# One last stage for epilogue and routed layer, and changed orders in self attention and the upward projection of a two-layer decoder

## The chip, the cores and the metric

The kernel runs on one core of a Trainium2 chip, as one launch. The metric is the device time of the execution in microseconds (us), the median of several runs of the same program. The engines are TensorE (PE in the rows; PEld is its weight load), VectorE (DVE), ScalarE (ACT), GpSimd (POOL) and SyncE (SP), which issues the DMAs. Each runs its own queue in order, and they wait for one another by semaphores.

## The reference, cut to what matters

The input x is 16 x 128 x 1024, and six sublayers follow one another, each with its residual and a layer norm:

```
x = _layernorm(x + _L0_attn_ref(x, ...))      # hydra: down, gelu, two mixers, gate, up
x = _layernorm(x + _L0_xattn_ref(x, ctx, ...))
x = _layernorm(x + _L0_ffn_ref(x, ...))
x = _layernorm(x + _L1_attn_ref(x, ...))      # self attention, rotary, 32 heads, 8 kv heads
x = _layernorm(x + _L1_xattn_ref(ctx, x, ...))# recurrent decoder over 128 steps
x = _layernorm(x + _L1_ffn_ref(x, ...))       # routed layer with a sign matrix
```

Of these, the diff touches the following lines:

```
alpha = jax.nn.sigmoid(gate1)                       # hydra's end
h = alpha * xmid + (1.0 - alpha) * h
h = xmid + h
h = h @ w_up.T + b_up
return x_init + jnp.transpose(h, (1, 0, 2))

att = jnp.where(causal, q k / sqrt(d), -inf)        # self attention, per head
out = (softmax(att) @ v) @ Wo

y = jnp.tanh(g @ L_gy_w.T + L_gy_b + s @ L_sy.T) @ L_yy_w.T + L_yy_b   # decoder, per step

routing = softmax(xf @ gate_w.T)                    # routed layer
out = xf * (routing @ in_channel_scale) @ sign(weight).T * (routing @ out_channel_scale) + bias
```

In the decoder, s and g of each step come from a recurrence; y depends on them alone, so it is made for all steps after the recurrence.

## The kernel before, in words

X, the 16 tiles of 128 rows x 1024, stays in SBUF through the whole kernel; a tile is one sequence, b from 0 to 15. PSUM is one tensor `ps` of eight banks of 512 floats. The stages follow one another. Each is a block in which every engine has a queue written out by hand; where a block ends, all engines meet, the stage's semaphores are cleared and all meet again (`Scope.release`, L48). `Chain` (L21) lets an engine wait for its own instruction by a semaphore.

All sublayers end in `Norm` (L64): VectorE forms the row (sum of product and X), `statistics` makes its mean and variance in three operations (L96, L99), GpSimd's `factors` makes scale and shift in four small ones (L106 to L109), and ScalarE's `apply` (L113) writes the normalised row to X. There are two row buffers; `row_free` counts the applied tiles (plus two).

**Hydra's end, L294 to L742.** The block "mx" (L295 on) runs two mixer layers. Its ScalarE begins with one exponential (L484), its VectorE with the setup of taps (L638 to L646), and then waits for TensorE's first projections. The block "up" (L677 on) makes the gate from `gate1` (ScalarE L690, VectorE L722 to L725), scales u (L726), mixes all sixteen tiles in one operation (L727) into `hm`, and then TensorE multiplies each tile by `w_up` and adds the bias (L712, L149), two banks for each tile in turn. VectorE forms the rows (L738).

**Self attention, L1287 to L1638.** For a tile b, TensorE (L1454 on) makes: scores of head group 0, the query projection of tile b+1 group 0, scores of group 1, query projection group 1, then for c = 0: four turns of probabilities (`turn_probs`, L1415, two banks in turn, 4 transposes each), `attend` (L1423); then the key (L1393) and value (L1398) projections of tile b+1; then `turn_probs` and `attend` for c = 1, the turned rows of tile b+2, and the output projection (L1438). ScalarE copies each turned piece out of PSUM (`keep_probs`, L1507), makes the exponentials (L1499) and copies keys and values (`keep_kv`, L1491 and L1492). `turn_probs` waits until the piece two before it is copied; `attend` until all four are.

**The decoder's epilogue, L2199 to L2269.** With all states `sh` and alignments `ah` kept, TensorE makes the tanh's arguments for four tiles at a time (L2218, L2221), ScalarE the tanh (L2241, into `hy`), and then for each tile TensorE makes y (L2229, two halves, with a bias product L149) into two banks, VectorE adds X (L2266), and the norm follows.

**The routed layer, L2277 to L2550.** For each tile: GpSimd copies the row out of X (L2349) and adds the bias to the copy (L2356), which waits for the row of the tile before; TensorE transposes the copy (L2375); the router's logits, softmax and a transposed routing follow (L2383 to L2507); input scales are a small product (L2399); VectorE multiplies (L2511), and three bf16 parts are split off in turn by ScalarE (L2458, L2460) and VectorE (L2514, L2516). The layer is 24 products for each half of 512 columns (L2412), into banks 4 and 5; the output scales (L2421) go to banks 6 and 7 and are kept by ScalarE (L2486). VectorE forms the row by L2542 and L2544 and only then (L2545) frees banks 4 and 5 and the bias rows. TensorE's order for tile b is: turned rows of b+1, output scales of b, route b+1, first half layer (with logits and turned routes of b+1 in it), input scales of b+1, second half layer. ScalarE's order is: output scales of b kept (L2486), split of b+1, kept rows and exponentials of b+2, `apply` of b. Before the loop ScalarE takes the sign of the eight weight tiles (L2477), which eight DMAs bring (L2335), and TensorE waits for all eight.

Of the kernel before, what the change touches and what calls it, by code (L numbers as in the profile page):

```python
# [163 lines left out]
def stage_hydra(nc, X, ps, ident, a):  # L164
    with ExitStack() as ctx:
# [128 lines left out]
        with ExitStack() as inner:  # L294
# [31 lines left out]
                "sq_done ssq_done rs_done rs_ready spread o_done o_kept u_done")  # L326
            UNITS = 4 * CH + 2
            CONV = (2 * CH, 2 * CH + 1)
            BANK = 4
            with nc.Block() as block:  # L330
# [306 lines left out]
                def _(dve):  # L637
# [10 lines left out]
                    dve.wait_ge(a_done, 1)  # L648
# [27 lines left out]
        with ExitStack() as inner:  # L676
# [4 lines left out]
            load, e_done, dve_seq, pool_seq, mixed, summed, freed = t.sems(  # L681
                "load e_done dve_seq pool_seq mixed summed freed")
            with nc.Block() as block:
# [4 lines left out]
                @block.scalar  # L688
                def _(act):
                    act.activation(gate[:, 1:2], gate[:, 0:1], ACT.Exp, scale=-1.0).then_inc(e_done, 1)  # L690
# [27 lines left out]
                def _(dve):  # L718
                    dve.wait_ge(e_done, 1)
                    link = Chain(dve, dve_seq)  # L720
                    al = gate[:, 2:3]
                    link(dve.tensor_scalar(al, gate[:, 1:2], 1.0, None, ALU.add))  # L722
                    link(dve.reciprocal(al, al))
                    link(dve.tensor_scalar(gate[:, 3:4], al, -1.0, 1.0, ALU.mult, ALU.add))
                    link(dve.tensor_scalar(al, al, 1.0, None, ALU.add))  # L725
                    link(dve.tensor_scalar(u[:, :], u[:, :], gate[:, 3:4], None, ALU.mult))  # L726
                    dve.scalar_tensor_tensor(out=hm[:, :, :].rearrange("p t s -> p s t"),  # L727
                                             in0=xmid[:, :].rearrange("p (s t) -> p s t", t=SEQ), scalar=al,
                                             in1=u[:, :].rearrange("p (s t) -> p s t", t=SEQ),
                                             op0=ALU.mult, op1=ALU.add).then_inc(mixed, 1)  # L730
# [1918 lines left out]
```

## Time and profile before

| | us |
|---|---|
| median of 3 runs (3503.76 to 3507.91) | 3505.43 |
| profiled execution, its own time | 3504.24 |
| its span | 3502.4 |
| upward projection, first product to last normalised row | 241.89 to 301.1 |
| self attention | 806 to 1595 |
| decoder's recurrence, up to its last operation | to 3153.8 |
| epilogue, first DMA to last normalised row | 3155.1 to 3226.9 |
| routed layer, first instruction to the end | 3228.0 to 3502.4 |

```
PE 3034.8 (87%) x42733; PEld 2061.2 (59%) x42778; DVE 1974.6 (56%) x5167; ACT 1699.7 (49%) x4978; POOL 288.1 (8%) x994
```

The shares are averages over stages with different limits: in each place that the change touches, what counts is which wait ends last there. The span is from the first to the last instruction; 1.8 us of the execution lie around it. In the timelines of the section below, a row has the start, the length, the engine, the line, the operation, output and inputs, shapes and count, and in brackets the idle time before it and what ended it. "L12" is line 12 of the kernel. A float32 product shows as two records.

### The profile page before, as it was taken

Reading aid. Unit: us, or ns where it says so; the run is one execution under the profiler, and the core shown is the slowest. Engines: PE = TensorE matmul, PEld = TensorE weight load, DVE = VectorE, ACT = ScalarE, POOL = GpSimd, SP = SyncE. Lnnn points to the kernel's source line nnn. Section 1 sums busy time; section 2 is a strip of 40 time slices with the busy share of each in tenths; the row PEclk is TensorE's granted clock in tenths of the full one; section 3 lists DMA queues with packets and bytes.
Section 4 is the critical chain, followed back from the end, with each engine's and each line's share of the span. In section 5 each row is a group of like instructions: output and inputs, shape, how many; then the busy total and the mean of one; then the engine's idle time right before and its main releaser. Section 6 shows DMA issues by size and latency. Waiting matters only on the chain. (4 is left out here: it accounts for less than half of the span.)

```text
span 3502.4 us, 107527 instructions
## 1 busy us (share of the span) xinstructions
PE 3034.8 (87%) x42733; PEld 2061.2 (59%) x42778; DVE 1974.6 (56%) x5167; ACT 1699.7 (49%) x4978; POOL 288.1 (8%) x994
## 2 busy tenths in 40 slices
PE   7876985667999999988989999999999999996898
PEld 4434552336777667754457677676767767762444
DVE  3776776885555555552035555555555555555454
ACT  2333544553444444441136666666666666653433
POOL 1002000000000000001000000000000000002232
PEclk8988997888999999999999999999999999998899
DMA  3002002001000000001123333333333333321100
GB/s 114 8 7 61 11 5 87 0 0 51 1 0 0 0 0 0 0 1 64 35 55 93 88 93 89 91 92 89 93 88 93 88 93 88 93 83 39 49 36 36
DMA packets 287962, 176.19 MB, mean 50 GB/s; under 512 B 23574, under 2 KB 277095, under 8 KB 287901
## 3 DMA queue, kind: packets, MB, share of 16 engines
q1 hardware_dynamic: 284860, 171.16, 16.7%
q0 software_dynamic: 3040, 4.23, 0.6%
q8 instruction: 37, 0.61, 0.1%
q14 instruction: 25, 0.20, 0.0%
HBM read 164.36 MB, written 14.16 MB: 51 GB/s over the span
## 5 line engine op out<-in xcount | busy, mean ns | idle before, releaser
L1987 PE MATMUL ps<-de_hg,st_at 128*32 128x128 f32 x16384 | 516.3, 275 | 0.3 <-DVE st_at L2148 0.3
L1987 PEld LDWEIGHTS ps<-de_hg,st_at 128*32 128x32 f32 x16384 | 424.4, 110 | 31.6 <-DVE st_at L2148 0.5
L2052 ACT ACTIVATE st_th<-ps,st_sw 128x128 f32<-128x128 f32 x1024 | 291.9, 368 | 237.5 <-PE ps L1959 237.5
L2131 DVE TENSOR_TENSOR st_th<-ps,st_sw 128x512 f32<-128x512 f32 x256 | 177.1, 692 | 162.3 <-PE ps L1959 162.3
L1380 PE MATMUL ps<-sa_xt,w_wq 128*128 128x128 f32 x2048 | 239.3, 278 | 0.8 <-ACT sa_xt L1481 0.8
L1380 PEld LDWEIGHTS ps<-sa_xt,w_wq 128*128 128x128 f32 x2048 | 233.5, 194 | 4.9 <-issue 1.4
L1948 PE MATMUL ps<-st_hk,de_cwt 112*32 112x128 f32 x4096 | 164.7, 278 | 79.7 <-DMA st_hk<-padded_alignments 76.1
L1438 PE MATMUL ps<-sa_wo,sa_ct 128*128 128x512 f32 x512 | 222.6, 593 | 0.0
L1499 ACT ACTIVATE sa_pr<-sa_pr,sa_nm 128x128 f32<-128x128 f32 x512 | 197.6, 389 | 7.6 <-DVE sa_nm L1585 7.6
L1959 PE MATMUL ps<-st_fs,de_waf 32*128 32x128 f32 x4096 | 186.5, 296 | 15.8
L2412 PE MATMUL ps<-rf_wb,rf_sp 128*128 128x512 bf16 x737 | 175.3, 385 | 16.9 <-DVEq L2545 15.3
L1948 PEld LDWEIGHTS ps<-st_hk,de_cwt 112*32 112x32 f32 x4096 | 100.2, 109 | 144.8 <-ACT st_gt L2071 94.3
L2125 DVE COPY ps<-de_enc 128x512 f32<-128x512 f32 x256 | 175.1, 684 | 5.9 <-PE ps L2021 5.9
L2162 DVE TENSOR_TENSOR st_rec<-ps,st_rin 128x128 f32<-128x128 f32 x256 | 74.7, 292 | 176.2 <-PE ps L1987 176.2
L1925 POOL COPY de_ah<-st_at 128x8 f32 (+1 forms) x256 | 50.7, 198 | 1444.1 <-DVE st_at L2148 1444.1
L1974 PE MATMUL ps<-st_th,st_vas 128*32 128x128 f32 x4096 | 165.3, 279 | 1.7 <-ACT st_th L2057 1.7
L1629 DVE TENSOR_TENSOR sa_row<-ps,X 128x512 f32<-128x512 f32 x32 | 22.1, 692 | 254.5 <-PE ps L1438 254.5
L2057 ACT ACTIVATE st_th<-st_th 128x512 f32<-128x512 f32 x256 | 165.2, 645 | 0.0
L1438 PEld LDWEIGHTS ps<-sa_wo,sa_ct 128*128 128x128 f32 x512 | 96.0, 190 | 116.5 <-issue 116.5
L2045 ACT COPY ps<-de_enc 128x512 f32<-128x512 f32 x256 | 156.8, 612 | 10.0 <-PE ps L2021 10.0
L1959 PEld LDWEIGHTS ps<-st_fs,de_waf 32*128 32x128 f32 x4096 | 137.7, 185 | 33.9 <-ACT st_fs L2042 30.5
L113 ACT ACTIVATE X<-sa_row,sa_rs_ln 128x1024 f32 (+1 forms) x16 | 19.9, 1242 | 274.5 <-POOL sa_rs_ln L109 274.5
(400 smaller groups left out, 5816.1 us busy)
## 6 DMA issues: line engine op xcount, KB each, us to landing
st_hk<-padded_alignments SPq DMA_DIRECT2D x254, 448.0 KB, 3.6
X<-in_x_dram SPq DMA_DIRECT2D x16, 512.0 KB, 8.1
out_dram<-X SPq DMA_DIRECT2D x16, 512.0 KB, 2.6
w_wq<-in_Wq_perm_dram SPq DMA_DIRECT2D x1, 4096.0 KB
sa_wo<-in_Wo_perm_dram SPq DMA_DIRECT2D x1, 4096.0 KB, 14.2
gate_inputs<-dp_ro SPq DMA_DIRECT2D x16, 256.0 KB, 2.3
st_rin<-gate_inputs SPq DMA_DIRECT2D x128, 32.0 KB, 3.2
rf_wf<-in_weightT_dram SPq DMA_DIRECT2D x8, 512.0 KB, 6.9
```

Of the source, the lines that this page charges most:

```text
L1380: ins = pe.matmul(ps[:, 6 + c, g * P:(g + 1) * P], wq[:, k, (4 * c + g) * P:(4 * c + g + 1) * P], xt[:, k, :], start=(k == 0), stop=(k == ...
L1438: ins = pe.matmul(ps[:, 6 + h, :], ct[:, k // 4, (k % 4) * P:(k % 4 + 1) * P], wo[:, k, h * 512:(h + 1) * 512], start=(k == 0), stop=(k == ...
L1499: ins = act.activation(pr[:, c, h, :], pr[:, c, h, :], ACT.Exp, bias=nm[:, c, h:h + 1], accum_out=sums[:, c, h:h + 1])
L1948: ins = pe.matmul(F[g][32 * j:32 * j + 32, :], cwt[:, i, :], hk[g][:, 2 * j + i, :], start=(i == 0), stop=(i == 1), tile_position=(0, 32 * ...
L1959: ins = pe.matmul(ps[:, j, c0:c0 + P], waf[32 * j:32 * j + 32, i, :], fs[g][32 * j:32 * j + 32, :], start=False, stop=True, tile_position= ...
L1974: ins = pe.matmul(E[g][32 * j:32 * j + 32, :], vas[:, i, :], th[g][:, 2 * j + i, :], start=False, stop=(i == 1), tile_position=(0, 32 * j) ...
L1987: ins = pe.matmul(R[g][32 * q:32 * q + 32, :], at[g][:, b, :], hg[:, BG * g + b, q * P:(q + 1) * P], start=False, stop=(b == BG - 1), tile ...
L2052: ins = act.activation(th[g][:, b, :], sums(g, 0)[:, b // 2, (b % 2) * P:(b % 2 + 1) * P], ACT.Tanh, bias=sw[g][:, b:b + 1])
L2057: act.activation(v, v, ACT.Tanh).then_inc(th_done[g], 1)
L2125: dve.tensor_copy(sums(g, 1), four(enc[:, BG * g + 4:BG * g + 8, :])).then_inc(filled1[g], 1)
L2131: dve.tensor_tensor(th[g][:, 4:8, :].rearrange("p (k s) n -> p k s n", s=2), sums(g, 1).rearrange("p k (s n) -> p k s n", s=2), sw[g][:, 4 ...
L2412: ins = pe.matmul(ps[:, 4 + h, :], sp3[:, k, part, m * P:(m + 1) * P], wb[:, m, h * 512:(h + 1) * 512], start=(n == 0), stop=(n == 3 * KH ...
```

## The change

It has four parts.

1. The gate. The exponential of the gate moves to the head of the block "mx" on ScalarE, and its four small VectorE operations with it, ahead of the two layers. There xmid is scaled by 1 + alpha, once. In "up", the scaling of u and the single mix are replaced by four operations of four tiles each, and TensorE waits for the one that it needs.
2. Self attention. `turn_probs` is split, and the projections of tile b+1 stand between its parts; ScalarE's copies are put in the same order.
3. Epilogue and routed layer are one stage. State products, tanh and the first three y tiles (AHEAD = 3) come first; the further y tiles are made inside the routed loop, three tiles ahead, between the input scales and the second half layer, in banks 6 and 7. A second `Norm` (`eln`) has its own rows. The weights `wf` have room for four tiles, and the last four DMAs wait for a sign each. The large decoder tensors are released before the stage, in a release of their own. TensorE's loop over the tiles is written out.
4. GpSimd's copy of a row and its bias addition are split, with the factors of the y row three ahead between them, and the copy waits until that tile's y row is applied.

The diff, cut to its core (indentation-only lines left out):

```diff
@@ mx, ScalarE and VectorE @@
 act.activation(nega[:, :], alog[:, :], ACT.Exp).then_inc(a_done, 1)
+act.activation(gate[:, 1:2], gate[:, 0:1], ACT.Exp, scale=-1.0).then_inc(a_done, 1)
...
-dve.wait_ge(a_done, 1)
+dve.wait_ge(a_done, 2)
+link(dve.tensor_scalar(al, gate[:, 1:2], 1.0, None, ALU.add))
+link(dve.reciprocal(al, al))
+link(dve.tensor_scalar(gate[:, 3:4], al, -1.0, 1.0, ALU.mult, ALU.add))
+link(dve.tensor_scalar(al, al, 1.0, None, ALU.add))
+link(dve.tensor_scalar(xmid[:, :], xmid[:, :], al, None, ALU.mult))
@@ up @@
-pe.wait_ge(mixed, 1)
 for b in range(NB):
+    pe.wait_ge(mixed, b // 4 + 1)
...
-link(dve.tensor_scalar(u[:, :], u[:, :], gate[:, 3:4], None, ALU.mult))
-dve.scalar_tensor_tensor(out=hm[:, :, :].rearrange("p t s -> p s t"),
...
+for c in range(CH):
+    rows = slice(4 * c, 4 * c + 4)
+    dve.scalar_tensor_tensor(out=hm[:, rows, :].rearrange("p t s -> p s t"),
...
@@ self attention, TensorE @@
-turn_probs(pe, b, 0, n0)
-attend(pe, b, k, 0, n0)
-if more:
-    for c in range(NC):
-        project_k(pe, b + 1, c)
-    project_v(pe, b + 1)
-turn_probs(pe, b, 1, n0 + QD)
+for c in range(NC):
+    turn_probs(pe, b, 0, n0, range(2 * c, 2 * c + 2))
+    if more:
+        project_k(pe, b + 1, c)
+attend(pe, b, k, 0, n0)
+turn_probs(pe, b, 1, n0 + QD, range(2))
+if more:
+    project_v(pe, b + 1)
+turn_probs(pe, b, 1, n0 + QD, range(2, QD))
 attend(pe, b, k, 1, n0 + QD)
@@ self attention, ScalarE @@
 keep_context(act, b, 0)
+keep_probs(act, b, 1, n0 + QD, range(2))
 if more:
     keep_kv(act, b + 1, 1 - k)
-keep_probs(act, b, 1, n0 + QD)
+keep_probs(act, b, 1, n0 + QD, range(2, QD))
@@ routed stage, SyncE @@
+for dst, src in ((lsy, "L_syT"), (gyb, "L_gy_b"), (lyy, "L_yyT")):
+    sp.dma_start(dst[:, :], a[src]).then_inc(yy_load, 16)
...
 for k in range(KH):
-    sp.dma_start(wf[:, k, :], a["weightT"][k * P:(k + 1) * P, :]).then_inc(wf_load[k // 2], 16)
+    if k == 4:
+        sp.dma_start(bias[:, :], a["bias"].partition_broadcast(P)).then_inc(bias_load, 16)
+    if k >= 4:
+        sp.wait_ge(signed, k - 3)
+    sp.dma_start(wf[:, k % 4, :], a["weightT"][k * P:(k + 1) * P, :]).then_inc(wf_load[k // 2], 16)
@@ GpSimd @@
+eln.start_pool(pool, link)
+ln.start_pool(pool, link)
+for b in range(2):
+    eln.factors(pool, link, b, b)
+for b in range(2):
+    stage_rows(b, b)
+eln.factors(pool, link, 2, 0)
+for b in range(2):
+    add_bias(b, b)
+def body(b, k, more):
+    link = state["link"]
+    if has(b + 2):
+        stage_rows(b + 2, k)
+    if has(b + AHEAD):
+        eln.factors(pool, link, b + AHEAD, 1 - k)
+    if has(b + 2):
+        add_bias(b + 2, k)
+    ln.factors(pool, link, b, k)
@@ TensorE @@
+def make_y(pe, b):
+    pe.wait_ge(hy_done, b // 4 + 1)
+    if b >= 2:
+        pe.wait_ge(y_used, b - 1 if b == 2 else b)
+    if b >= AHEAD:
+        pe.wait_ge(os_kept, b - AHEAD + 1)
+    for h in range(2):
+        out = ps[:, y_bank(b) + h, :]
+        pe.matmul(out, hy[:, b, :], lyy[:, h * 512:(h + 1) * 512], start=True, stop=False)
+        ins = y_bias.add(pe, out, h)
+    ins.then_inc(y_rows, 1)
...
     if more:
         input_scales(pe, b + 1, 1 - k)
+    if b + AHEAD < NB:
+        make_y(pe, b + AHEAD)
     layer(pe, b, k, 1)
@@ ScalarE @@
+eln.apply(act, 0, 0)
+eln.apply(act, 1, 1)
 keep_rows(act, 0)
+signs(range(0, 2))
 exps(act, 0)
+signs(range(2, 4))
 split(act, 0, 0)
+eln.apply(act, 2, 0)
+signs(range(4, KH))
...
     ln.apply(act, b, k)
+    if has(b + AHEAD):
+        eln.apply(act, b + AHEAD, 1 - k)
@@ VectorE @@
+def y_row(dve, link, b, k):
+    n = y_bank(b) if isinstance(b, int) else 6
+    dve.wait_ge(y_rows, b + 1)
+    eln.wait_free(dve, b)
+    link(dve.tensor_tensor(eln.row[:, k, :], ps[:, n:n + 2, :].rearrange("p a n -> p (a n)"), tile_of(b), ALU.add))
+    dve.sem_inc(y_used, 1)
...
 dve.tensor_tensor(r1[:, :], ys[:, :], sp3[:, k, 0, :], ALU.subtract).then_inc(r_done, 1)
+if between is not None:
+    between()
...
-        scale_rows(dve, link, b + 1, 1 - k)
+        ahead = has(b + AHEAD)
+        scale_rows(dve, link, b + 1, 1 - k, (lambda: y_row(dve, link, b + AHEAD, 1 - k)) if ahead else None)
+        if ahead:
+            eln.statistics(dve, link, 1 - k)
```

## Rows read from the trace of the kernel before

**Rows 1.** Busy time by stretch: epilogue, and routed loop; columns name start:end and length first.

```profile
3172.40:3221.20 48.80, 34.97 (x89) 12.89 (x88) 42.30 (x76) 17.36 (x14) 14.98 (x57) 0.99 0.00 0
3283.00:3473.00 190.00, 176.73 (x1244) 94.71 (x1269) 108.15 (x169) 75.80 (x116) 56.37 (x77) 1.00 0.09 36
```

**Rows 2.** One tile of the routed loop: timeline; last its rows' DVE group.

```profile
3270.84 1.89 PE L2412 MATMUL ps<-rf_wb,rf_sp 128*128 128x512 bf16 x7 [0.85 <-DVEq L2545]
3270.85 2.35 POOL L2356 TENSOR_TENSOR rf_xb<-rf_xs,rf_bias 128x1024 f32<-128x1024 f32 x1 [19.26 <-DVEq L2545]
3274.51 1.24 ACT L113 ACTIVATE X<-rf_row,rf_rs_ln 128x1024 f32 x1 [1.07 <-POOL rf_rs_ln L109]
3275.66 0.99 ACT L2486 COPY rf_os<-ps 128x1024 f32<-128x1024 f32 x1
3276.36 0.73 PE L2399 MATMUL ps<-rf_rT,rf_ics 8*128 8x128 f32 x16
3277.01 5.35 PE L2412 MATMUL ps<-rf_wb,rf_sp 128*128 128x512 bf16 x23
3277.15 1.23 DVE L2511 TENSOR_TENSOR rf_ys<-ps,rf_xt 128x1024 f32<-128x1024 f32 x1 [1.26 <-PE ps L2399]
3279.56 1.23 DVE L2514 TENSOR_TENSOR rf_r<-rf_ys,rf_sp 128x1024 f32<-128x1024 f32 x1 [1.18 <-ACT rf_sp L2458]
3283.04 1.22 DVE L2542 TENSOR_TENSOR rf_row<-ps,rf_os 128x1024 f32<-128x1024 f32 x1
L2542 DVE TENSOR_TENSOR rf_row<-ps,rf_os x16: 1217/1218/1225, 3268.2 to 3491.4; 128x1024 f32<-128x1024 f32 x16
```

**Rows 3.** Head of the upward projection: timeline, and the weights' DMA (last: us to landing).

```profile
238.04 3.70 DVE L727 SCALAR_TENSOR_TENSOR up_hm<-hy_xmid,hy_gate,hy_u 128x2048 f32<-128x2048 f32 x1
241.89 2.04 PE L712 MATMUL ps<-up_w_up,up_hm 128*128 128x512 f32 x2 [10.96 <-DVE up_hm L727]
up_w_up<-in_w_upT_dram SPq DMA_DIRECT2D x1, 512.0 KB, 4.1
```

**Rows 4.** Timeline of one self-attention tile, TensorE: start us, us.

```profile
1095.26 1.04 PE L1419 MATMUL ps<-identity,sa_pr 128*128 128x128 f32 x8
1099.48 3.84 PE L1393 MATMUL ps<-sa_xt,w_wk 128*128 128x128 f32 x32
1106.61 1.04 PE L1419 MATMUL ps<-identity,sa_pr 128*128 128x128 f32 x8
1109.83 1.06 PE L1427 MATMUL ps<-sa_pt,sa_vv 128*32 128x512 f32 x8 [0.68 <-ACT sa_pt L1507]
```

**Rows 5.** The same tile, ScalarE timeline.

```profile
1107.34 1.09 ACT L1507 COPY sa_pt<-ps 128x512 f32<-128x512 f32 x2
```

**Rows 6.** Timeline of the epilogue's first tiles.

```profile
3172.10 1.02 PE L2229 MATMUL ps<-yy_lyy,yy_hy 128*128 128x512 f32 x2
3173.18 1.02 PE L2229 MATMUL ps<-yy_lyy,yy_hy 128*128 128x512 f32 x2
3173.78 1.42 DVE L96 BATCH_NORM_STATS2 yy_stats<-yy_row 128x6 f32<-128x512 f32 x2
3175.52 1.22 DVE L2266 TENSOR_TENSOR yy_row<-ps,X 128x1024 f32<-128x1024 f32 x1
3179.68 0.19 POOL L109 TENSOR_TENSOR yy_rs_ln<-yy_vy,yy_rs_ln 128x1 f32<-128x1 f32 x1
```

**Rows 7.** Timeline behind a stage that ends with two releases.

```profile
302.77 1.28 ACT L889 ACT_TABLE_LOAD   x1 [1.68 <-PEq L51]
```

**Rows 8.** Timeline of the routed layer's head, from its first row copy.

```profile
3228.49 1.04 POOL L2349 COPY rf_xs<-X 128x1024 f32<-128x1024 f32 x1
3244.73 3.89 ACT L2477 ACTIVATE rf_wb<-rf_wf 128x1024 bf16<-128x1024 f32 x4
3248.96 1.96 PE L2375 MATMUL ps<-identity,rf_xs 128*128 128x128 f32 x8 [11.32 <-ACT rf_wb L2477]
```

**Rows 9.** Timeline at the last tile, TensorE.

```profile
3479.07 12.21 PE L2412 MATMUL ps<-rf_wb,rf_sp 128*128 128x512 bf16 x47 [2.21 <-DVEq L2545]
```

More of the change, by code:

```diff
@@ L680, in stage_hydra @@
             ln = Norm(t, X)
-            load, e_done, dve_seq, pool_seq, mixed, summed, freed = t.sems(
-                "load e_done dve_seq pool_seq mixed summed freed")
+            load, dve_seq, pool_seq, mixed, summed, freed = t.sems(
+                "load dve_seq pool_seq mixed summed freed")
             with nc.Block() as block:
@@ L1412, in scores, with turn_probs @@
                 ins.then_inc(s_sum, 1)
-            def turn_probs(pe, b, c, n0):
-                for r in range(QD):
+            def turn_probs(pe, b, c, n0, rs):
+                for r in rs:
                     pe.wait_ge(normed, QD * (2 * b + c) + r + 1)
@@ L1501, in exps, with keep_probs @@
                     ins.then_inc(exp_done, 1)
-            def keep_probs(act, b, c, n0):
-                for r in range(QD):
+            def keep_probs(act, b, c, n0, rs):
+                for r in rs:
                     act.wait_ge(tp_done, n0 + r + 1)
@@ L2315, in over_tiles @@
         def over_tiles(eng, body, start=lambda i: None):
-            with eng.Fori(0, NB // 2 - 1) as i:
+            with eng.Fori(0, NB // 2 - 2) as i:
                 start(i)
@@ L2319, in over_tiles, with has @@
                 body(2 * i + 1, 1, True)
-            start(NB // 2 - 1)
-            body(LAST - 1, 0, True)
-            body(LAST, 1, False)
+            start(NB // 2 - 2)
+            for b in range(NB - 4, NB):
+                body(b, b % 2, b < LAST)
+        def has(b):
+            return not isinstance(b, int) or b <= LAST
         with nc.Block() as block:
@@ L2347, in stage_rows, with add_bias @@
                         pool.wait_ge(biased, b - 1)
-                    if not (isinstance(b, int) and b == 1):
-                        pool.tensor_copy(xs[:, k, :], tile_of(b)).then_inc(staged, 1)
+                    pool.wait_ge(eln.row_free, b + 3)
+                    pool.tensor_copy(xs[:, k, :], tile_of(b)).then_inc(staged, 1)
+                def add_bias(b, k):
                     if not (isinstance(b, int) and b < 2):
                         pool.wait_ge(row_done, b - 1)
+                    else:
+                        pool.wait_ge(bias_load, 16)
@@ L2352, in stage_rows @@
                     pool.wait_ge(staged, b + 1)
-                    if isinstance(b, int) and b == 0:
-                        pool.tensor_copy(xs[:, 1, :], tile_of(1)).then_inc(staged, 1)
-                        pool.wait_ge(bias_load, 16)
                     pool.tensor_tensor(xb[:, k, :], xs[:, k, :], bias[:, :], ALU.add).then_inc(biased, 1)
-                ln.start_pool(pool, Chain(pool, pool_seq))
-                stage_rows(0, 0)
-                stage_rows(1, 1)
-                with pool.Fori(0, NB // 2 - 1) as i:
-                    link = Chain(pool, pool_seq, ln.POOL_SETUP + i * 2 * ln.POOL_LINKS)
-                    for k in range(2):
-                        stage_rows(2 * i + k + 2, k)
-                        ln.factors(pool, link, 2 * i + k, k)
@@ L2370, in turn_rows, with start @@
+                state = {}
+                def start(i):
+                    state["link"] = Chain(pool, pool_seq, SETUP + i * 4 * ln.POOL_LINKS)
+                over_tiles(pool, body, start)
             def turn_rows(pe, b, k):
@@ L2435, in _ @@
                 pe.wait_ge(signed, KH)
-                def body(b, k, more):
+                pe.wait_ge(y_used, AHEAD)
+                for b in range(NB):
+                    k, more = b % 2, b < LAST
                     if more:
@@ L2488, in body @@
                         split(act, b + 1, 1 - k)
-                    if not isinstance(b, int) or b < LAST - 1:
+                    if has(b + 2):
                         keep_rows(act, b + 2)
@@ L2521, in _ @@
                 dve.memset(rt[:, :, :], 0.0).then_inc(cleared, 1)
+                dve.wait_ge(yy_load, 48)
+                dve.tensor_scalar(lsy[:, :], lsy[:, :], 0.5, None, ALU.mult).then_inc(halved, 1)
                 link = Chain(dve, dve_seq)
+                for b in range(AHEAD):
+                    y_row(dve, link, b, b % 2)
+                    eln.statistics(dve, link, b % 2)
                 softmax_top(dve, 0)
```

1057 lines of the change are left out of this document (508 added, 549 removed).

## The prediction

> **What bounds the kernel now.** I read the timeline of each place that the diff touches, and the busy times by stretch for its clock. In the epilogue stage VectorE is busy for 42.30 of 48.80 us [rows 1]: a tile costs it a row addition and statistics, while TensorE only makes two short products, so tiles pass at VectorE's pace. In the routed loop TensorE is busy for 176.73 of 190.00 us at a granted clock of 1.00, and VectorE for 108.15 [rows 1]; the starts of the sixteen row multiplications, 3268.2 to 3491.4, are (3491.4 - 3268.2) / 15 = 14.88 us apart [rows 2]. In each tile TensorE waits 0.85 us for the row of the tile before [rows 2]. So one stage leaves TensorE room and the other leaves room to VectorE and ScalarE; to run them together is worth what the slower engine of each hides. In self attention TensorE bounds, and what can go is only its waits for ScalarE's copies. In the upward projection the first product stands still until one operation of 3.70 us has mixed all sixteen tiles [rows 3].
>
> **Upward projection.** Before, the first product starts at 241.89, behind the mix that starts at 238.04 [rows 3]. After, the gate's five small operations and the scaling of xmid are done in the mixing stage, and the mix is four operations, of which the first takes about 3.70 / 4 = 0.93 us. The product then waits for its weights: they are asked for at the stage's start, 234.4, and land 4.1 us later [rows 3], at 238.5. Gain 241.89 - 238.6 = 3.3 us; the rest of that stage is paced by VectorE as before and moves with it. The moved operations stand in VectorE's queue ahead of its first convolution, which waits for a projection of TensorE; I cost them at nothing, since TensorE has to run two groups of projections first. Without that cover they cost some 2 us. Bounds: 0 (quartered rows are costly, or that cover is gone) to 3.9 (the weights earlier).
>
> **Self attention, fifteen tiles.** From the first turned probabilities at 1095.26 to the second attend at 1109.83 a tile takes 14.57 us [rows 4]. TensorE's work in it is four pairs of turns at 1.03 and one attend at 1.0 (1.04 and 1.06 in the rows, less what the next one overlaps), and the key and value projections, 1106.61 - 1099.48 = 7.13 [rows 4]: 12.25 us. The waits are 2.32. The new order puts one key projection (1.8) between the first two pairs of turns, the other before the attend, and the value projection between the last two. Each is longer than the 1.09 us of a pair of copies [rows 5], so three of four waits go. What stays is the last: ScalarE copies keys and values, then two pieces of probabilities. In the trace this string ends at 1107.34 + 1.09 = 1108.43, that is 1.82 after the value projection's issue ends at 1106.61 [rows 4, 5]; TensorE has only one pair of turns (1.03) to fill it and some 0.1 for the semaphore, an estimate: it waits 1.82 + 0.1 - 1.03 = 0.89. Gain 2.32 - 0.89 = 1.43 a tile, 15 x 1.43 = 21.3 (the last tile has no projections). ScalarE now waits for the third turn behind the key projection, so the exponentials behind it come about 2 us later; the value projection gives their consumer more room than that. Bounds: 0.5 a tile (they are late after all) to 2.32, that is 8 to 35 us.
>
> **Tail, the head of the new stage.** The state products and the first two y rows run as before. The first row copy of the routed layer can follow the second tile's factors, which end at 3179.68 + 0.19 = 3179.87 [rows 6]; an added release ahead of the stage, bounded by nothing and by the 1.68 us that ScalarE sat behind two of them [rows 7], I take at 0.4. So the copy starts at 3180.3 where it was at 3228.49 [rows 8]: 48.2 us earlier. From the copy to the loop it was 3248.96 - 3228.49 = 20.5 us [rows 8], a string of ScalarE's copies, splits and eight signs (the last four 3.89). I keep that length: weights now land under the y rows, which removes a wait, and the third row's normalisation of 1.24 comes in. The last four weight tiles wait for a sign each, with more than 10 us before their use; SyncE's stores of the result, queued behind them, begin only with the first finished row. A table for tanh that lacks the exponential or the sign would add a load of 1.28 [rows 7]. Bounds 17 to 24.
>
> **Tail, the loop.** Call H the start of a tile's first half layer, 3270.84 [rows 2]. The y product adds two halves of 3173.18 - 3172.10 = 1.08 us [rows 6], so 2.15, behind the input scales, which end at 3276.36 + 0.73 = H + 6.25. It also waits until ScalarE has kept the output scales, for they share two banks. That copy starts at 3275.66, H + 4.82, and takes 0.99 [rows 2]. Ahead of it in ScalarE's queue there is now one more normalisation of 1.24 (the same operation at 3274.51 [rows 2]), so it ends at H + 7.05. The y product starts at H + 7.1, a new wait of 0.9, and ends at H + 9.25; the second half layer of 5.35 [rows 2] ends at H + 14.6, and VectorE's row can start at H + 14.74. VectorE's own string: before, its row starts at 3283.04, H + 12.20 [rows 2]. Put in are the y row, which the epilogue shows at 1.22 [rows 6] and which with its own semaphore I take at 1.37; it begins when the subtraction at 3279.56 ends and covers the wait for the cast (the last operation comes 0.27 later); and a tile's statistics, 3175.52 - 3173.78 = 1.74 [rows 6]: H + 14.21. So TensorE's side is last by half a us. From row to next H it is 14.88 - 12.20 = 2.68, and the period is 14.74 + 2.68 = 17.42, 2.54 more. Twelve tiles pay that; the first, where no normalisation stands ahead of that copy, pays 2.0; the last three pay nothing. Together 32.5. Bounds per tile: 2.0 (no wait for the copy) to 3.6 (a row copy of 1.04 on top). GpSimd's queue gets a second set of factors between its copy and its bias addition; that addition starts with the row at H anyway [rows 2], and the factors are ready two us earlier. The added release at the end: 0.4, same bounds.
>
> **The page that speaks against it.** GpSimd's row copy, 1.04 us [rows 8], now waits for the normalised y row and falls at H + 6.2 to H + 7.2; VectorE's subtraction with two SBUF inputs starts at 3279.56, H + 8.7 [rows 2]. They are 1.5 us apart; no row shows the two together. The Trainium skill (SBUF — State Buffer, section "SBUF: two separate sides") says that GpSimd and such an operation of VectorE exclude one another for the whole instruction. By that the sum stays, as long as ScalarE is not 1.5 us later than I work out; if it is, rival B below.
>
> **Sum.** -3.3 - 21.3 - 48.2 + 32.5 + 0.4 = -39.9. The profiled execution took 3504.24 us (span 3502.4), so 3464.3; the median of the runs lies 1.2 above it: 3465.5 us.
>
> **Rivals.** *A, no wait for the output scales:* ScalarE's normalisations come earlier than I think. Against it: the tile's normalisation waits for GpSimd, whose bias addition of 2.35 starts at H [rows 2]. 12 x (2.54 - 2.01) = 6.4 less: 3459. *B, the copy and the subtraction meet:* 13 x 1.04 = 13.5 more: 3479. For it: ScalarE's queue is longer by 1.24 in each tile. *C, self attention gains only 8:* the later exponentials delay the last two normalised pieces. Against it: they have the whole value projection, over 3 us, as room. 13 more: 3479. *D, self attention loses all its waits:* 0.89 x 15 = 13.4 less: 3452. Against it the string of four copies above. *E, slower:* TensorE's clock falls in the loop. A pause of 0.85 leaves it at 1.00 [rows 1, 2]; behind the pause of 2.21 at the last tile 47 matmuls took 12.21 [rows 9] where two halves at the loop's pace are 10.7, so one fall costs 1.5. If both pauses of a tile (before the y product and before H) grow to 2.2, a tile pays 1.3 + 1.9 of pause and 3.0 of clock, 13 x 6.2 = 81 more: 3546. It decides from 39.9 / 13 = 3.1 us a tile. Against it: I find pauses of 0.9 and 0.3. *F, an edit does not take effect:* the upward product waits elsewhere, or the quarter mixes are slow: 3469.
>
> **How the numbers follow.** Forecast 0.48, A 0.12, B 0.12, C 0.12, D 0.05, E 0.05, F 0.06. The likeliest gives 3465.5. The range 3450 to 3486 takes in A to D and F, A with D for its lower end (3446 is left out) and B or C with a head at its long bound for its upper; E and mixtures of the rest are outside. A measurement of this kernel can tell about 0.2%, 7 us, from no change. Every case but E is faster by more; with something for a mixture that ends near zero: faster 0.92, within 0.02, slower 0.06.
>
> **What would show it.** In self attention the waits of the attend on the copies halve, to about 0.9 a tile, and the tile is 1.4 shorter. The first upward product starts near 238.6, released by its DMA. The first row copy of the routed layer is near 3156, where the earlier stages' 25 us are off. Routed rows 17.4 apart, with a wait of 0.9 ahead of the y product, released by ScalarE's copy of the output scales; 16.9 would be A, 18.5 B. A clock below 1.00 in the loop would be E. If the tile of self attention keeps its length, the order was not what cost.

## The result, and the profile after

The changed kernel takes **3460.55 us** (median of 4 runs, 3457.25 to 3462.39); the kernel before, run beside it, 3506.67 (4 runs, 3503.76 to 3514.15). The ratio is 0.9864, 95% interval 0.9848 to 0.9880: about 46 us faster. The forecast was 3465.5, in a range from 3450 to 3486. The profiled execution took 3461.36 us with a span of 3459.6, against 3504.24 and 3502.4.

The difference of the two spans, 42.8 us, by marks that both traces have (a set-up operation at the start of the mixing stage, the first transfer of each later stage, the last product of the decoder recurrence with the state weights):

| stretch | before | after | difference |
|---|---|---|---|
| start to the mixing stage | 65.8 | 62.8 | -3.0 |
| mixing stage | 168.6 | 167.9 | -0.7 |
| upward projection to the start of self attention | 575.4 | 572.6 | -2.8 |
| self attention and what follows, to the recurrence | 970.9 | 944.1 | -26.8 |
| decoder recurrence, 128 steps | 1367.7 | 1376.4 | +8.7 |
| recurrence to the first transfer of the tail | 6.7 | 7.1 | +0.4 |
| tail, from there to the end | 347.3 | 328.7 | -18.6 |

Two of these lie where no edit is: the 3.0 us ahead of the mixing stage, and 8.7 us lost in the recurrence. The experiments come back to both. The lines of the changed kernel are shifted by a few; the text names operations.

**Upward projection.** Timeline of its head in the kernel after (start us, us, engine, line, operation, output<-input, in brackets the idle time before and what ended it); it answers to [rows 3]:

```profile
230.74 0.37 SPq L695 DMA_DIRECT2D up_w_up<-in_w_upT_dram  x1
230.79 3.86 DVE L729 SCALAR_TENSOR_TENSOR up_hm<-hy_u,hy_gate,hy_xmid 128x512 f32<-128x512 f32 x4 [1.06 <-PEq L51]
234.46 2.08 PE L720 MATMUL ps<-up_w_up,up_hm 128*128 128x512 f32 x2 [7.22 <-DMA up_w_up<-in_w_upT_dram]
```

The four quarter mixes take 3.86 us together, 0.16 more than the one of 3.70 did. The product is now released by its weights and starts 3.72 us after they are asked for (234.46 - 230.74).

**Self attention.** Timeline of one tile, TensorE and the last copies of ScalarE; it answers to [rows 4, 5]:

```profile
1079.86 1.04 PE L1421 MATMUL ps<-identity,sa_pr 128*128 128x128 f32 x8
1080.73 2.02 PE L1395 MATMUL ps<-sa_xt,w_wk 128*128 128x128 f32 x16
1082.58 1.04 PE L1421 MATMUL ps<-identity,sa_pr 128*128 128x128 f32 x8
1083.46 1.95 PE L1395 MATMUL ps<-sa_xt,w_wk 128*128 128x128 f32 x16
1085.34 1.06 PE L1429 MATMUL ps<-sa_pt,sa_vv 128*32 128x512 f32 x8
1086.33 1.09 PE L1421 MATMUL ps<-identity,sa_pr 128*128 128x128 f32 x8
1087.26 3.62 PE L1400 MATMUL ps<-w_wv,sa_xt 128*128 128x256 f32 x16
1090.72 1.04 PE L1421 MATMUL ps<-identity,sa_pr 128*128 128x128 f32 x8
1091.45 1.09 ACT L1511 COPY sa_pt<-ps 128x512 f32<-128x512 f32 x2
1092.60 1.07 PE L1429 MATMUL ps<-sa_pt,sa_vv 128*32 128x512 f32 x8 [0.84 <-ACT sa_pt L1511]
```

The stretch that was 14.57 us is 12.74 (1092.60 - 1079.86), and one bracket is left in it: 0.84 us ahead of the second attend, behind the copies that end at 1092.54.

**Tail.** Timeline of the head; it answers to [rows 6 to 8]. The second line is the first row of the former epilogue, the third the first row copy of the routed layer, the last the start of the loop:

```profile
3130.87 1.28 ACT L2474 ACT_TABLE_LOAD   x1 [1.68 <-PEq L51]
3147.08 1.23 DVE L2532 TENSOR_TENSOR yy_row<-ps,X 128x1024 f32<-128x1024 f32 x1 [11.33 <-PE ps L149]
3154.29 1.04 POOL L2301 COPY rf_xs<-X 128x1024 f32<-128x1024 f32 x1
3170.55 3.88 ACT L2486 ACTIVATE rf_wb<-rf_wf 128x1024 bf16<-128x1024 f32 x4
3174.48 1.97 PE L2345 MATMUL ps<-identity,rf_xs 128*128 128x128 f32 x8 [9.68 <-ACT rf_wb L2486]
```

The one table load of the tail is that first line: the table serves tanh, exponential and sign alike. Between the row copy and the loop stand these, in order of time (GpSimd's two bias additions, the last two operations of VectorE's softmax, and ScalarE's first cast, which starts the split of the tile):

```profile
3157.87 4.65 POOL L2309 TENSOR_TENSOR rf_xb<-rf_xs,rf_bias 128x1024 f32<-128x1024 f32 x2
3160.49 0.17 DVE L2522 RECIPROCAL rf_ri<-rf_sm 128x1 f32<-128x1 f32 x1 [0.42 <-ACT rf_ex L2470]
3160.69 1.86 DVE L2523 TENSOR_SCALAR rf_rt<-rf_ex,rf_ri 128x32 f32<-128x32 f32 x1
3166.12 1.04 ACT L2461 CAST rf_sp<-rf_ys 128x1024 bf16<-128x1024 f32 x1 [3.77 <-DVE rf_ys L2537]
```

VectorE's scaling of the softmax takes 1.86 us here and 0.24 in every other tile and in the kernel before. It ends at 3162.55, GpSimd's additions at 3162.52. Next, one tile of the loop, which answers to [rows 2], and the group of its sixteen rows:

```profile
3267.75 1.89 PE L2382 MATMUL ps<-rf_wb,rf_sp 128*128 128x512 bf16 x8 [0.22 <-DVEq L2582]
3271.43 1.24 ACT L113 ACTIVATE X<-rf_row,rf_rs_ln 128x1024 f32 x1 [1.08 <-POOL rf_rs_ln L109]
3272.58 1.23 ACT L113 ACTIVATE X<-yy_row,yy_rs_ln 128x1024 f32 x1
3273.71 0.99 ACT L2503 COPY rf_os<-ps 128x1024 f32<-128x1024 f32 x1
3273.97 1.04 POOL L2301 COPY rf_xs<-X 128x1024 f32 x1 [2.67 <-ACT X L113]
3274.84 1.10 PE L2419 MATMUL ps<-yy_lyy,de_hgy 128*128 128x512 f32 x2 [0.85 <-ACT rf_os L2503]
3276.46 1.22 DVE L2540 TENSOR_TENSOR rf_r<-rf_ys,rf_sp 128x1024 f32<-128x1024 f32 x1 [1.18 <-ACT rf_sp L2461]
3277.07 5.34 PE L2382 MATMUL ps<-rf_wb,rf_sp 128*128 128x512 bf16 x24
3282.45 1.22 DVE L2579 TENSOR_TENSOR rf_row<-ps,rf_os 128x1024 f32<-128x1024 f32 x1 [0.67 <-PE ps L2382]
L2579 DVE TENSOR_TENSOR rf_row<-ps,rf_os x16: 1217/1224/1226, 3195.7 to 3448.4; 128x1024 f32<-128x1024 f32 x16
```

With H = 3267.75 the y product waits 0.85 us for ScalarE's copy of the output scales and starts at H + 7.09; the row starts at H + 14.70, with 0.67 us of room for VectorE. The forecast had H + 7.1 and H + 14.74. The thirteenth row starts at 3403.83, so twelve periods take (3403.83 - 3195.70) / 12 = 17.34 us each. The busy times of 200 us of this loop (stretch, length, busy us of PE, PEld, DVE, ACT, POOL, granted clock, DMA share, GB/s; compare [rows 1]):

```profile
3213.00:3413.00 200.00, 188.56 (x1233) 97.46 (x1232) 128.46 (x209) 82.27 (x118) 64.78 (x118) 1.00 0.08 32
```

TensorE is busy for 94% of it at a granted clock of 1.00 (the 2.4 GHz level): rival E did not come.

### The profile page after: what moved, and what is told of

It reads as the page before. It is cut to its first block and busy times, and to the rows that moved or that the text cites. A ratio compares the mean times of both kernels' runs of the same rounds, so it can differ in the third digit from the quotient of the medians.

```text
span 3459.6 us, 107419 instructions
## 1 busy us (share of the span) xinstructions
PE 3027.8 (88%) x42778; PEld 2061.6 (60%) x42778; DVE 1975.7 (57%) x5170; ACT 1693.2 (49%) x4976; POOL 288.2 (8%) x994
## 5 line engine op out<-in xcount | busy, mean ns | idle before, releaser
L1994 PE MATMUL ps<-dm_hg,st_at 128*32 128x128 f32 x16384 | 516.3, 275 | 0.3 <-DVE st_at L2155 0.3
L1994 PEld LDWEIGHTS ps<-dm_hg,st_at 128*32 128x32 f32 x16384 | 424.5, 110 | 31.6 <-DVE st_at L2155 0.5
L1955 PE MATMUL ps<-st_hk,dm_cwt 112*32 112x128 f32 x4096 | 164.7, 278 | 87.1 <-DMA st_hk<-padded_alignments 83.8
L1966 PE MATMUL ps<-st_fs,dm_waf 32*128 32x128 f32 x4096 | 186.5, 296 | 14.0
L1955 PEld LDWEIGHTS ps<-st_hk,dm_cwt 112*32 112x32 f32 x4096 | 100.3, 109 | 152.1 <-ACT st_gt L2078 104.9
L2132 DVE COPY ps<-dm_enc 128x512 f32<-128x512 f32 x256 | 175.0, 684 | 5.9 <-PE ps L2028 5.9
L2052 ACT COPY ps<-dm_enc 128x512 f32<-128x512 f32 x256 | 156.8, 613 | 10.1 <-PE ps L2028 10.1
L1966 PEld LDWEIGHTS ps<-st_fs,dm_waf 32*128 32x128 f32 x4096 | 137.7, 185 | 30.9 <-ACT st_fs L2049 26.5
```

The source lines that it names most:

```text
L1955: ins = pe.matmul(F[g][32 * j:32 * j + 32, :], cwt[:, i, :], hk[g][:, 2 * j + i, :], start=(i == 0), stop=(i == 1), tile_position=(0, 32 * ...
L1966: ins = pe.matmul(ps[:, j, c0:c0 + P], waf[32 * j:32 * j + 32, i, :], fs[g][32 * j:32 * j + 32, :], start=False, stop=True, tile_position= ...
L1994: ins = pe.matmul(R[g][32 * q:32 * q + 32, :], at[g][:, b, :], hg[:, BG * g + b, q * P:(q + 1) * P], start=False, stop=(b == BG - 1), tile ...
L2132: dve.tensor_copy(sums(g, 1), four(enc[:, BG * g + 4:BG * g + 8, :])).then_inc(filled1[g], 1)
```

## Experiments

### The three parts alone

The kernel before with one stage's edit each: the self attention order; the mixing stage and upward projection; the merged last stage with the freed arrays of the recurrence. Each takes the diff's hunks of its stage as they stand.

> Only the order in self attention is changed. My theory: that stage alone is 27 us shorter, as the kernel after shows, of which the first forecast took 21, so the time is near 3479 (ratio 0.9923), and the decoder recurrence is as in the kernel before (1367.6 us). Rival: the stage carries a part of what the other edits gave, and alone it is worth the forecast 21 us (0.9939).

**Measured:** 3475.87 us against 3501.32, ratio 0.9920 (0.9905 to 0.9935). From the first transfer of self attention to the recurrence it took 943.8 us (970.9 before). The stage earns its 27 us alone.

> Only the mixing stage and the upward projection are changed. My theory: the first upward product is released by its weights near 4 us after the stage starts (3.72 in the kernel after) instead of 7.5, the stage from its start to the start of cross attention takes 64.3 us instead of 68.3, and the run is about 4 us faster (ratio 0.9989), with the decoder recurrence as before (1367.6 us from its weight load to its last filter product). Rival: the 3.0 us by which the kernel after is already ahead when the mixing starts come from the change too, and the run is 7 us faster. Second rival: later stages wait for something else and give it back, 0 to 2 us faster.

**Measured:** 3501.58 us against 3501.32, ratio 0.9999 (0.9990 to 1.0008). In its profile the first product starts 3.7 us after the stage's first transfer, and from that transfer to self attention it took 570.5 us. The whole runs spread over 12 us for the kernel before alone (3495.39 to 3507.98); their interval leaves room for a gain of at most 3.5 us, so the forecast of 4 for the whole missed. The stage shows more: over all profiles of this study that stretch took 574.1 to 576.4 us in the six without the edit (mean 575.7) and 569.7 to 572.6 in the eight with it (mean 571.4). The edit is worth 4.3 us there. A part seems to be given back behind self attention, as the second rival has it: from the last normalised row of that stage to the first transfer of the recurrence the six took 188.8 to 189.0 us, and the eight 189.0 to 189.1 in three cases and 190.5 to 191.4 in five (mean 190.2, so 1.4 more). That would leave 2.9 of the 4.3 us, which the whole runs allow. Why those five are longer was not tried. Of the first rival the profiles leave nothing: the mixing stage began at 59.6 to 65.9 us and took either about 164 or about 168 us, with the edit and without.

> Only the merged last stage, with the arrays of the decoder recurrence freed ahead of it. My theory: from the end of the recurrence to the end the kernel takes 330.4 us instead of 348.6, so 18 us faster; the recurrence, whose instructions are unchanged, takes as long as in the kernel before, and its 8.7 us more in the kernel after was a variation of its transfers from run to run: ratio 0.9948. Rival: the changed placement of the arrays costs the recurrence the 8.7 us, and the run is only 9 to 10 us faster (0.9973).

**Measured:** 3481.78 us against 3501.32, ratio 0.9940 (0.9926 to 0.9953). The tail took 329.1 us from its first transfer, the recurrence 1369.1. Together the three ratios make 0.9860, the whole change 0.9864: the parts add up.

### Half of the self attention order

The kernel with the new order, but:

```
-                    for c in range(NC):
-                        turn_probs(pe, b, 0, n0, range(2 * c, 2 * c + 2))
-                        if more:
-                            project_k(pe, b + 1, c)
+                    turn_probs(pe, b, 0, n0, range(QD))
                     attend(pe, b, k, 0, n0)
+                    if more:
+                        for c in range(NC):
+                            project_k(pe, b + 1, c)
```

> Half of the self attention order: the first four turns of probabilities stay together ahead of their attend, both key projections follow it, and only the value projection lies between the two last pairs of turns. My theory: the wait of the first attend for ScalarE's copies stays, the waits inside the second four turns go, and the stage is 12 to 16 us shorter than before instead of 27. Rival: ScalarE's string is what bounds the tile, one place for the copies is as good as the other, and nearly all of the 27 us is there already; or nothing, because the string only moves into the second attend.

**Measured:** 3494.86 us, ratio 0.9980 (0.9970 to 0.9989); 964.2 us to the recurrence, so 6.7 less than before. The waits of TensorE from 900 to 1500 us, some thirteen tiles; first the kernel before, then this one, then the kernel after (what waited <- for what: us in total, times, longest):

```profile
PE ps L1427 <- ACT sa_pt L1507: 18.6, 26, 0.8
PE ps L1419 <- ACT sa_pt L1507: 8.4, 26, 0.4
```

```profile
PE ps L1427 <- ACT sa_pt L1509: 20.8, 26, 0.8
PE ps L1419 <- ACT sa_pt L1509: 3.8, 13, 0.3
```

```profile
PE ps L1429 <- ACT sa_pt L1511: 11.0, 13, 0.8
```

All three theories miss: 6.7 us is neither 12 to 16, nor nearly 27, nor nothing. Before, a tile waits (18.6 + 8.4) / 13 = 2.08 us; with the value projection moved 1.89; with the key projections moved too 0.85. The value projection takes one wait of 0.3 away ahead of a pair of turns, and the attend behind it still waits: the string of four copies comes after it in either order. With the value projection moved, moving the key projections brings the other 20 of the 27 us; they were not moved alone.

### The last wait of the self attention tile

The first half of the output projection's first column half needs only the first context, which has been kept by then:

```
                     turn_probs(pe, b, 1, n0 + QD, range(2, QD))
+                    project_out(pe, b, not more, True)
                     attend(pe, b, k, 1, n0 + QD)
                     if more2:
                         turn_rows(pe, b + 2, n0 + 2 * QD)
-                    project_out(pe, b, not more)
+                    project_out(pe, b, not more, False)
```

(True: products k = 0 to 3 of h = 0; False: the rest.)

> The kernel after, with the first four products of a self attention tile's output projection (3.6 us, they need only the first context) between the last turns and the last attend. My theory: the last wait of TensorE in the tile, 0.84 us for ScalarE's copies, goes, no other takes its place, and the stage is 15 x 0.84 = 12.6 us shorter; ratio near 0.9828. Rival: the second half of the projection now waits for the second context, or the next tile for its rows, and the tile keeps its length.

**Measured:** 3446.49 us against 3505.28, ratio 0.9833 (0.9819 to 0.9846); 932.6 us to the recurrence, so 11.5 less than after (forecast 12.6). The stage itself gains more: from its first transfer to its last normalised row it took 741.8 us instead of 755.1, so 13.3 less, and 1.8 were lost behind it, where this profile is one of the five with a long stretch (190.8). Of all the tiles between 900 and 1500 us TensorE now has one wait, and it is elsewhere:

```profile
PE ps L1444 <- ACT sa_ct L1522: 0.8, 1, 0.8
```

### The order of ScalarE in the routed loop

```
                     act.copy(os[:, :], ...).then_inc(os_kept, 1)
+                    if has(b + AHEAD - 1):
+                        eln.apply(act, b + AHEAD - 1, k)
...
                     ln.apply(act, b, k)
-                    if has(b + AHEAD):
-                        eln.apply(act, b + AHEAD, 1 - k)
```

and the call for the third row in the head goes.

> The kernel after, with ScalarE keeping the output scales of a routed tile ahead of the normalised y row instead of behind it (the third y row's normalisation moves from the head into the first tile with it). My theory: the wait of 0.85 us ahead of the y product goes, VectorE's string becomes the bound, whose wait for the layer of 0.67 us is used up, and the routed rows are 16.7 us apart instead of 17.34; with 12 tiles the tail is 8 us shorter (329 from its first transfer to about 321), ratio near 0.9841. Rival: the normalised row and with it GpSimd's row copy come 1 us later and meet VectorE's subtraction; the period stays near 17.3. And if the decoder recurrence here is near 1369.5 us as in the four kernels before this one, its 1376.4 in the kernel after was one run's own.

**Measured:** 3451.33 us against 3505.28, ratio 0.9843 (0.9829 to 0.9858). Its interval overlaps that of the kernel after; the tail decides: 319.0 us instead of 328.7, where 8 less were forecast. A tile of its timeline, and the group of its rows:

```profile
3262.87 1.89 PE L2382 MATMUL ps<-rf_wb,rf_sp 128*128 128x512 bf16 x8 [0.51 <-DVEq L2581]
3268.59 1.24 ACT L113 ACTIVATE X<-yy_row,yy_rs_ln 128x1024 f32 x1
3269.04 1.12 PE L2419 MATMUL ps<-yy_lyy,de_hgy 128*128 128x512 f32 x2
3269.99 1.04 POOL L2301 COPY rf_xs<-X 128x1024 f32 x1 [3.57 <-ACT X L113]
3271.59 1.23 DVE L2539 TENSOR_TENSOR rf_r<-rf_ys,rf_sp 128x1024 f32<-128x1024 f32 x1 [1.19 <-ACT rf_sp L2461]
3276.87 1.23 DVE L2578 TENSOR_TENSOR rf_row<-ps,rf_os 128x1024 f32<-128x1024 f32 x1
L2578 DVE TENSOR_TENSOR rf_row<-ps,rf_os x16: 1207/1225/1225, 3193.2 to 3438.4; 128x1024 f32<-128x1024 f32 x16
```

The y product has no bracket, and neither has VectorE's row: VectorE is last now. The thirteenth row is at 3393.87, the period (3393.87 - 3193.22) / 12 = 16.72 us. Twelve times 0.62 are 7.4 us; the rest of the 9.7 is in the head (19.05 us from the first row copy to the loop instead of 20.19) and in the first tile (20.2 instead of 21.2). GpSimd's row copy still ends 0.6 us ahead of VectorE's subtraction, so the rival did not come.

### The copy and the subtraction made to meet

```
                     pool.wait_ge(eln.row_free, b + 3)
+                    if not (isinstance(b, int) and b < 2):
+                        pool.wait_ge(hi_done, b)
                     pool.tensor_copy(xs[:, k, :], tile_of(b)).then_inc(staged, 1)
```

(`hi_done` is the signal of ScalarE's cast for which VectorE's subtraction waits.)

> The kernel after, with one wait more: GpSimd's row copy (1.04 us) starts when VectorE's subtraction of two SBUF rows (1.22 us) starts, 2.5 us later than now. By the Trainium skill (SBUF — State Buffer, section SBUF: two separate sides) one of them is held for the other's whole length: the subtraction at 2.2 us, or the copy starting with its end, and where it is the subtraction the tile is 0.6 us longer (VectorE has 0.67 us of room), 8 us in all. Rival: both run at their own lengths, 1.22 and 1.04, the period stays 17.34 and the ratio 0.9864.

**Measured:** 3460.17 us, ratio 0.9864 (0.9844 to 0.9883), the same as the kernel after. One tile of its timeline:

```profile
3274.56 1.23 DVE L2542 TENSOR_TENSOR rf_r<-rf_ys,rf_sp 128x1024 f32<-128x1024 f32 x1 [1.19 <-ACT rf_sp L2463]
3274.75 1.93 POOL L2303 COPY rf_xs<-X 128x1024 f32 x1 [5.36 <-ACT rf_sp L2463]
3275.70 1.22 DVE L2534 TENSOR_TENSOR yy_row<-ps,X 128x1024 f32<-128x1024 f32 x1
```

The subtraction keeps its 1.23 us. The copy, begun 0.19 later, takes 1.93 instead of 1.04, and so do all fourteen copies that wait for the signal (1.90 to 1.99): it loses 0.89 of the 1.04 us in which they overlap (3274.75 to 3275.79). So the two do hold each other off, and here it is GpSimd that pays; neither the 8 us that the theory put on VectorE nor the copy at its own length came. It had time to: the rows are still 17.3 to 17.4 us apart. Beside the y row, which reads PSUM and one row of SBUF, the copy goes on: it ends at 3276.68, within it.

### Both improvements together

> The kernel after with both edits, ScalarE's order in the routed loop and the early output products in self attention. They lie in different stages, so the sum: 20 us less than the kernel after, near ratio 0.9806. Rival: one of them gives nothing, 8 or 12 us less.

**Measured:** 3433.06 us against 3505.28, ratio 0.9801 (0.9785 to 0.9817). That is 0.6% below the kernel after, with intervals that do not touch, and the fastest kernel of this study. 932.3 us to the recurrence and 319.5 in the tail: each edit keeps its worth.

### What lengthened the recurrence

No edit touches its instructions. Two pairs of edits, the kernel after without one of its three parts, and last the kernel before again:

> Both earlier edits, the last two stages as before; read for the length of the decoder recurrence, whose instructions no edit touches. Five kernels with at most one edit took 1367.7 to 1370.2 us from its weight load to its last product, five with all three 1373.4 to 1376.4. Theory 1: the extra 5 us goes with something that the edits shift together (the place of code or of arrays), and a pair has it too, 1373 or more in at least one of the three pairs. Theory 2: it needs all three, and the pairs show 1368 to 1371. Beside it: stages as sums, so the upward projection 4.4 us shorter and self attention 27 us, near 3471 in all.

**Measured:** 3479.95 us in its one run; the recurrence 1375.7, self attention to recurrence 946.0.

> The kernel after without the edit of mixing stage and upward projection. Against the kernel after it should be 4 us slower by the stages: near ratio 0.9876 if the upward edit is worth what its stage shows, 0.9864 if it is worth nothing as the whole runs of it alone said. The recurrence: theory 1 of the pair before, 1373 or more; theory 2, 1368 to 1371.

**Measured:** 3458.2 us against 3504.3, ratio 0.9864 (0.9842 to 0.9885), too wide to tell 4 us; the recurrence 1373.1.

> The kernel after without the self attention order; read for the length of the recurrence, with the same two theories: 1373 us or more, or 1368 to 1371. The rest as sums: 4.4 and 18 us shorter than before.

**Measured:** 3478.72 us in its one run; the recurrence 1371.4.

> The kernel before once more, unchanged, as a control for the length of the decoder recurrence. Its one profile so far has 1367.7 us; the kernels that ran on one chip with at most one edit have 1369.1 to 1370.2, those on two other chips with two or three edits 1371.4 to 1376.1, so edits and chips are mixed up. Theory 1, it goes with the edits: 1367 to 1370 again. Theory 2, it goes with the chip and the run: some other value, and if it is 1373 or more this alone shows that no edit is needed for it. On the chip of the first four this run could not tell them apart.

**Measured:** 3502.72 us in its one run, the recurrence 1373.8. The group rows that give this length, first to last start at the ends: the load of the state weights and the last product with them, for the kernel before again and then for the kernel after:

```profile
L1980 PE MATMUL ps<-st_lss,st_sT x2048: 272/273/298, 1790.8 to 3149.0; 128*32 128x128 f32 x187
L1893 SPq DMA_DIRECT2D st_lss<-in_L_ssT_dram x1: 361/361/361, 1775.2 to 1775.2; - x1
```

```profile
L1987 PE MATMUL ps<-st_lss,st_sT x2048: 272/273/298, 1763.0 to 3123.8; 128*32 128x128 f32 x187
L1900 SPq DMA_DIRECT2D st_lss<-in_L_ssT_dram x1: 362/362/362, 1747.4 to 1747.4; - x1
```

The unchanged kernel has 1367.7 us in one profile and 1373.8 in another. No edit is needed for at least 6.1 of the 8.7 us. So the three pairs, which came out as theory 1 has it (1373 or more in two of them), do not show that edits are the cause; and the 1369.5 us expected of the kernel with ScalarE's order turned missed, for it had 1376.1. By chips: 1369.1 to 1370.2 for the four kernels on the first, 1373.4 to 1376.1 for the four on the second, 1371.4 to 1375.7 for the three on the third. A step of the recurrence waits for a transfer that goes out to memory and comes back, and of TensorE's waits in the recurrence the one for it grows most: 76.1 us in the first profile of the kernel before, 80.6 in the second, 83.8 in the kernel after. Whether the chip or the single run sets it stays open; so does a share of the edits of up to the 2.6 us between 1373.8 and 1376.4.

## Why the prediction was right

**Upward projection, -3.3 forecast.** Right. The product started 3.72 us after its weights were asked for where 4.2 was taken, and the stretch is 2.8 us shorter in the profiled pair and 4.3 by the means of all profiles. That a later stretch might give 1.4 of it back was not foreseen. The five moved operations cost nothing that shows: the mixing stage took the same two lengths with and without them.

**Self attention, -21.3 forecast, -26.8 measured.** The cause was right, a term was mis-sized. The wait that was to stay, 0.89, measured 0.84. The work did not come to 12.25 us but to 12.74 - 0.84 = 11.90: I charged each pair of turns its 1.03 us, and where a projection follows without a wait it takes over after 0.87, 0.88 and 0.93. For the kernel before I took the waits as what is left, 2.32, where its brackets add up to 2.08: the rest was time in which a pair of turns could not overlap with what follows, because that had to wait. So a tile gains 14.57 - 12.74 = 1.83 us and not 1.43: 2.08 - 0.85 = 1.23 are brackets, and 0.6 is that overlap, which I had only in part. Rival C (later exponentials) and rival D (no wait left) did not come; the experiment with the early output products shows that D would be worth about 13 us, and that it takes another 3.6 us of work in that place.

**Head, -48.2 forecast.** From the last product of the recurrence to the first row copy it was 80.1 us (3148.4 to 3228.5) and is 30.5: -49.6. The added release cost its 0.4 (6.7 to 7.1). Of the 1.4 more, 1.2 are the state products: from the first of them to the first y product it took 8.84 us (3135.89 to 3144.73) where it was 10.02. Their granted clock is 0.62 from 3138 to 3140 and 1.00 from there on; in the kernel before it stayed at 0.50 and 0.51 from 3160 to 3166. I had them unchanged.

From copy to loop I kept 20.5 us; it is 20.19. The number holds, the account does not. The third row's normalisation (1.24) came in and the waits for weights (2.10 and 0.54) went, as argued, but ScalarE's string does not set the length: its first cast waits 3.77 us for VectorE's scaled row. That chain goes back, through two small products and a copy that wait for one another, to the softmax's scaling, which did not end before GpSimd's bias additions did. I looked for such a meeting at the row copy in the loop only. All eight kernels with the merged stage show it: the scaling takes 1.04 or 1.86 us instead of 0.24, ends 0.03 to 0.04 us behind the second bias addition, which itself ends 8.2 us behind the start of the first row copy, and the six with the forecast order of ScalarE take 20.19 or 20.20 us from copy to loop, whichever of the two it is. So a hold of 0.80 to 1.62 us is in the head. What the head would be without it was not run; that it came out so near to 20.5 is luck.

**Loop, +32.5 forecast.** Measured 273.95 us from its start to the last row (3174.48 to 3448.43) where it was 242.4: +31.5. The first tile pays 21.2 - 19.2 = 2.0 as forecast, twelve tiles 17.34 - 14.88 = 2.46 where I had 2.54, and the last three, 14.8 to 15.0 us, nothing. The term of 0.4 for the release at the end measured 0.2. The new wait was forecast at 0.9 with its place and its releaser; it is 0.85 and has both. That it cost time, and that VectorE stood 0.5 us behind it, is shown by the kernel without it: 16.72 us, the pace that VectorE allows.

**Rivals.** A came true only where I made it true, with ScalarE's order turned. B failed twice over: the copy and the subtraction do not meet, and where they are made to, with the subtraction 0.19 us ahead, the price falls on GpSimd's copy and not on the path. F: the product is released by its weights and the quarter mixes are not slow. E: both pauses are there (0.85 and 0.22) and the clock stays at 1.00; behind the last tile's pause, which the change leaves alone, the halves run as slowly as before:

```profile
3436.13 12.21 PE L2382 MATMUL ps<-rf_wb,rf_sp 128*128 128x512 bf16 x48 [2.21 <-DVEq L2582]
```

**The sum.** Forecast -39.9; the edited stretches of the profiled pair give -2.8 - 26.8 + 0.4 - 18.6 = -47.8. The stretches without an edit and the mixing stage gave 5.0 of that back in the pair (-3.0 - 0.7 + 8.7), which leaves -42.8. So the edits were worth 7.9 us more than forecast, most of it in self attention, and that 3465.5 lies only 5 us from 3460.55 is in part luck: an unchanged recurrence ran longer. The median fell by 46.1.

## What to carry to other kernels

When two stages are run together, write the queue of each engine for one tile with start times before building it; the new wait came out to 0.05 us that way, and it named the two operations of ScalarE to swap for another 9.7 us. Write that queue for the head of the stage too, with GpSimd's long operations in it: the meeting that the forecast did not have was there and not in the loop. Where an engine waits for copies of its own results, look for work that needs none of them and put a piece between each production and its use: the value projection in one piece of 3.5 us was worth 6.7 us in the stage, the key projections in two pieces of 1.9 us, placed beside it, another 20. Judge an edit of 4 us in a kernel of 3500 by the length of its stage over several profiles, since whole runs of one kernel differ by 12, look whether a stage behind it gives some of it back, and look at an unchanged stage before blaming the change for it.

## What the hardware showed beside

A GpSimd copy of 128x1024 that starts with a VectorE subtraction of two SBUF rows loses 0.89 of 1.04 us of overlap while the subtraction loses nothing. The Trainium skill (SBUF — State Buffer, section "SBUF: two separate sides") says that the one that starts first keeps the shared port for its whole length and the other waits; the trace agrees for VectorE first, with 0.89 us.

With GpSimd first the price falls on VectorE, and on a much smaller operation: a scaling of 128x32 that takes 0.24 us alone took 1.86 beside a GpSimd addition of two SBUF rows, begun before it, and ended 0.03 us behind it. A reciprocal of 128x1 kept its 0.17 us beside the same addition (3160.49). In both directions the profiler books the lost time in the length of the operation that is held and not as idle time before it, so no bracket names it: compare an operation's length with its other tiles.

The decoder recurrence, 128 steps that each go out to memory and back, took 1367.7 and 1373.8 us in two profiles of the same kernel. The mixing stage took either 163.5 to 164.6 or 167.9 to 168.6 us, never between, with and without the edit; what decides it was not tried.
